# The scan layer's tile loop, six turns of two tiles, written out on all five engines

## The reference, cut to what matters

```
h = x @ fc1_w.T + fc1_b
xc, z = split(h @ in_proj_w.T, 2)            # 512 inner channels each
u = silu(causal_conv4(xc) + conv_b)
dt_low, Bm, Cm = split(u @ x_proj_w.T)       # 16, 16 states, 16 states
dt = softplus(dt_low @ dt_proj_w.T + dt_proj_b)
A = -exp(A_log)
hstate = exp(dt_t * A) * hstate + (dt_t * u_t) * B_t     # along the 2048 rows
y_t = einsum('bdn,bn->bd', hstate, C_t)
y = (y + u * D) * silu(z)
s = (y @ out_proj_w.T) @ fc2_w.T + fc2_b
g = silu((silu(xn @ wg.T) * (xn @ wu.T)) @ wd.T)
out = x + s * silu_of_ffn                    # silu_of_ffn = g above
```

## Time and profile before

| what | value |
|---|---|
| three timed runs | 3019.51, 3020.09, 3027.25 us, median 3020.09 |
| profiled execution | 3014.55 us |
| its span, from first to last instruction | 3012.9 us |
| scan layer in it | 1015 to 3012 us |
| busy over the span | PE 86%, DVE 77%, POOL 69%, ACT 67% |
| instruction queues | 127 and 109 packets, 2.08 and 0.89 MB |
| mean granted PE clock in the scan layer | 0.97 of full speed |

### The profile page before, as it was taken

How to read it: one execution, slowest core, us unless ns; L and a number is a source line. 1 busy time by engine, 2 the same in 40 slices (tenths; PEclk the granted TensorE clock), 3 DMA queues, 4 the chain that set the end, 5 groups by cost and what they waited for, 6 DMA issues and landing times.

```text
span 3012.9 us, 43961 instructions
## 1 busy us (share of the span) xinstructions
PE 2588.0 (86%) x13290; PEld 1488.0 (49%) x13290; DVE 2306.4 (77%) x2777; ACT 2027.6 (67%) x3268; POOL 2069.9 (69%) x650
## 2 busy tenths in 40 slices
PE   6776188888887769998999899999899899999987
PEld 2333033333333435564665555656556566566455
DVE  6577466556562269989889799898798888989995
ACT  3221146656564379878788698797787887978874
POOL 0454430000000179999999899999899999999996
PEclk9998579989998879999999999999999999999999
DMA  8335497767641123032132130321312303213210
GB/s 274 105 103 127 109 266 210 186 175 180 172 140 46 55 120 120 30 119 100 36 120 85 65 120 33 117 99 36 121 52 97 120 17 126 105 38 120 78 63 7
DMA packets 133934, 323.21 MB, mean 107 GB/s; under 512 B 13233, under 2 KB 89009, under 8 KB 117314
## 3 DMA queue, kind: packets, MB, share of 16 engines
q1 hardware_dynamic: 113186, 248.84, 26.7%
q0 software_dynamic: 19200, 70.73, 7.1%
q10 hardware_dynamic: 1312, 0.66, 0.1%
HBM read 277.12 MB, written 43.13 MB: 106 GB/s over the span
## 4 chain that ended last, share of the span: by engine, by line
PE 26%; issue 12%; POOL 12%; ACT 7%; DVE 7%; ACTq 1%; DVEq 1%; DMA 0%; POOLq 0%; SPq 0%
PE l_p_w L1995 11%; PE l_p_y L1987 6%; POOL l_st L1638 5%; PE l_p_w L2041 5%; DVE l_st L1457 4%; POOL l_st L1630 3%; PE l_p_w L2060 3%; ACT l_p_a L1716 2%; POOL keep_xg L1638 2%; DVE keep_xg L1457 1%; ACT L1791 1%; POOL l_dtu L1644 1%; ACT L1725 1%; DVE keep_xg L1466 1%; PE l_p_w L2017 1%
## 5 line engine op out<-in xcount | busy, mean ns | idle before, releaser
L1457 DVE TENSOR_TENSOR_SCAN l_st<-l_p_a,l_hl,l_st 128x512 f32<-128x512 f32 x768 | 931.6, 1265 | 112.1 <-ACT l_p_a L1716 93.0
L1638 POOL TENSOR_TENSOR l_st<-l_st,l_cs 128x2048 f32<-128x2048 f32 x192 | 868.6, 4541 | 4.1 <-ACT l_hl L1721 3.8
L1716 ACT ACTIVATE l_p_a<-l_dt,lw_a_neg 128x512 f32<-128x512 f32 x1024 | 666.1, 681 | 51.6 <-DVE keep_xg L1457 40.4
L1630 POOL TENSOR_TENSOR l_st<-l_bs,l_dtu 128x2048 f32<-128x2048 f32 x128 | 580.9, 4539 | 47.5 <-PE l_p_y L1987 44.2
L1987 PEld LDWEIGHTS l_p_y<-keep_ident,l_st 128*128 128x128 f32 x3072 | 353.8, 144 | 136.9 <-POOL l_st L1638 74.8
L1987 PE MATMUL l_p_y<-keep_ident,l_st 128*128 128x128 f32 x3072 | 382.4, 281 | 42.9 <-POOL l_st L1638 42.9
L977 ACT ACTIVATE a_pr<-a_p_s 128x512 f32<-128x512 f32 x512 | 284.8, 596 | 163.9 <-PE a_p_s L1043 145.7
L901 DVE TENSOR_REDUCE a_mpart<-a_p_m 128x1 f32<-128x512 f32 x512 | 315.2, 683 | 98.2 <-PE a_p_m L1008 96.5
L1457 DVE TENSOR_TENSOR_SCAN keep_xg<-l_p_a,l_hl,keep_xg 128x512 f32<-128x512 f32 x256 | 314.8, 1267 | 2.3 <-DVE keep_xg L1466 1.9
L1638 POOL TENSOR_TENSOR keep_xg<-keep_xg,l_cs 128x2048 f32<-128x2048 f32 x64 | 290.7, 4542 | 11.0 <-ACT l_hl L1721 11.0
L1043 PE MATMUL a_p_s<-a_qst,kx 99*128 99x256 bf16 x1024 | 206.7, 292 | 73.6 <-ACT a_pr L977 54.8
(11 more groups left out here) (225 smaller groups left out, 3920.1 us busy)
## 6 DMA issues: line engine op xcount, KB each, us to landing
a_w<-in_w_dram POOLq DMA_DIRECT2D x64, 1024.0 KB, 12.0
l_bs<-s_bc SPq DMA_DIRECT2D x64, 1024.0 KB, 4.7
l_cs<-s_bc SPq DMA_DIRECT2D x64, 1024.0 KB, 4.9
keep_share<-s_x SPq DMA_DIRECT2D x32, 512.0 KB, 4.4
s_kp<-t_kp SPq DMA_DIRECT2D x96, 128.0 KB
kx<-s_kp SPq DMA_DIRECT2D x16, 768.0 KB, 11.8
s_vp<-t_vo SPq DMA_DIRECT2D x16, 544.0 KB
a_vg<-s_vp SPq DMA_DIRECT2D x16, 544.0 KB, 11.7
```

The costliest lines, as they stand in the source:

```text
L1457: eng.tensor_tensor_scan(st[k % NG][:, n, :], p_a[:, n, :], st[k % NG][:, n, :], hl[:, k, n:n + 1], ALU.mult, ALU.add).then_inc(scan_ok, 1)
L1630: eng.tensor_tensor(st[n][:, :, :], bs[:, 4 * n:4 * n + 4, :], dtu[(k // NG) % 2][:, :].unsqueeze(1).broadcast_to([P, NG, TT]), ALU.mult). ...
L1638: eng.tensor_tensor(st[n][:, :, :], st[n][:, :, :], cs[:, 4 * n:4 * n + 4, :], ALU.mult).then_inc(cm_ok, 1)
L1716: eng.activation(p_a[:, n, :], dt[c % 2][:, :], ACT.Exp, scale=a_neg[:, c, m:m + 1]).then_inc(dA_ok, 1)
```

## The change

The loop is gone. All 19 periods, -1 to 17, are written out by a loop of the program that builds the kernel, so that q is a plain number everywhere. For each q the four flags and the parity have the same values as before; on each engine the operations of a period and their order are the same.

```diff
--- before.py
+++ after.py
@@ -66,16 +66,8 @@
 
 def tiles(eng, period):
 
-    period(-1, 1, False, False, False, True)
-    period(0, 0, True, False, False, True)
-    period(1, 1, True, True, False, True)
-    with eng.Fori(0, (NT - 4) // 2) as j:
-        for p in range(2):
-            period(j * 2 + (2 + p), p, True, True, True, True)
-    period(NT - 2, 0, True, True, True, True)
-    period(NT - 1, 1, True, True, True, False)
-    period(NT, 0, False, True, True, False)
-    period(NT + 1, 1, False, False, True, False)
+    for q in range(-1, NT + 2):
+        period(q, q % 2, 0 <= q < NT, 1 <= q <= NT, 2 <= q, q + 1 < NT)
```

## The result

| | before | after |
|---|---|---|
| median of the timed runs | 3023.67 us (4 runs, 3019.51 to 3027.87) | 2975.09 us (4 runs, 2972.40 to 2976.80) |
| profiled execution, its span | 3014.55, 3012.9 us | 2973.50, 2971.8 us |

The ratio of after to before is 0.9838, with a 95% interval from 0.9818 to 0.9859: faster by 1.6%.

A forecast was written before the change was run, and what follows sets the result against it. POOL, almost without slack, was taken to bound the scan layer. Jumps 30.4 and register work 11.0 (41.35 by row spacing) plus 0.6 for period 2 gave 42 us: 3020.1 - 42.0 = 2978 us, range 2967 to 2991.

The forecast's parts named there:

- POOL sets the pace, and the written-out tiles 14 and 15 are the measure: Scan layer: POOL is busy 115.39 of 118.10 us per loop tile; the twelve loop tiles should become like periods 14 and 15.
- Jumps, 30.4 us: Scan loop: five jumps back stall PE and lengthen their tiles by 3.3 to 9.7 us each; all 30.4 us go.
- Register work, 1.03 us a tile: Scan loop tiles: computed waits and their arithmetic cost 118.06 - 117.03 us per tile, 11.0 us over eleven tiles.
- Period 2's first half, 0.6 us: Before the first residual row counted: POOL's wait should fall from 2.40 to 1.77 us, gaining 0.6.
- Straight code costs nothing to fetch: Twelve new written-out tiles: instruction traffic falls and no fetch stall is added, as in tiles 14 and 15; cost zero.
- rival (c): Slower: PE stalls at 16 KB packet ends in straight code, 48 packets, 149 us against 42 gained, 3127 us; chance 0.04.
- the DVE row: Straight code: one unexplained 3.00 us on DVE, taken as costing nothing; far bound 36 us if all twelve tiles exposed one.
- (a): Scan tiles: only the jumps go, the 1.03 us per tile stays; gain 30.4 us, time 2990; chance 0.06.
- (b): Scan layer: PE's stalls come from something else at a new turn and stay; gain 11.6 us, time 3008; chance 0.03.
- The clock: Granted PE clock: expected to lose its dip to 0.96 in the tile with the longest stall.
- the tile that was named: The scan loop tile with the longest PE stall, 5.09 us; the tile takes 127.71 us.
- The base: Whole kernel: the 42.0 us gain was put against the median 3020.1 of three timed runs, giving 2978.

The follow-up runs named there:

- PE's loop alone: Against the kernel before: PE keeps the loop of six turns, the four other engines are written out; 3011.42 us, ratio 0.9976.
- four periods a turn: Against the kernel before: three turns of four periods on every engine instead of six of two; 2997.12 us, ratio 0.9927.
- the hint: Kernel before, loop kept, plus one instruction per turn and engine naming the jump back ahead of time; 2987.47 us, ratio 0.9901.
- ACT's loop alone: Against the kernel before: ACT keeps the loop of six turns, the four other engines are written out; 2987.89 us, ratio 0.989.

## Why the prediction was right, by its own steps

- **POOL sets the pace, and the written-out tiles 14 and 15 are the measure.** Right: 117.03 us expected for each tile, 117.03 measured; 41.35 us for the eleven, 41.33 measured.
- **Jumps, 30.4 us.** Right in size and bearer, and shown three ways: PE's loop alone makes the five tiles as long again, two jumps instead of five (four periods a turn) cost 12 us instead of 30, and the hint removes it. Of the five engines it is PE's jump alone that costs much; the prediction had read that from the rows but not claimed it. One part of the mechanism it left unsaid: the stalls are 21.3 of the 30.4 us. The rest is the lower clock level at four of the five jumps, where PE does half the work. Stall plus half of that stretch gives 4.8, 6.5, 3.4, 10.2 and 6.6 us (an estimate from the trace), and the tiles' excess over 118.06 is 4.79, 6.36, 3.34, 9.65 and 6.21. With four periods a turn it gives 5.1 and 6.6, where the tiles exceed their neighbours by 5.1 and 6.6; with PE's loop alone it gives 1.3 to 1.6 us too much at four of five jumps.
- **Register work, 1.03 us a tile.** The gain per tile was right, its make-up was not. The bearer was not named: I argued over PE's wait, but PE's own share is zero; it waits for ACT's copy. ACT's loop alone costs 0.83. And a loop tile without a stretch at the lower clock level takes only 117.7, so the register work by itself is 0.7; the other 0.3 comes only where such a stretch falls into a loop tile. The 0.83 of ACT alone is more than the 0.7 of all five engines together, so the parts don't add up exactly.
- **Period 2's first half, 0.6 us.** The wait fell by 0.62 as said, but the row came 1.44 earlier. The rest stands ahead of it, in code that the change doesn't touch, and it is scatter: in the ten kernels whose attention stage is the same, this first row lies between 1224.76 and 1229.87.
- **Straight code costs nothing to fetch, rival (c).** Right: no stall over 1 us in twelve more tiles, on any engine, but the DVE row, which is there again at its old place (2.99 us). It is not open any more:

```profile
2838.65 4.55 POOL L1622 TENSOR_TENSOR l_st<-l_bs,l_dtu 128x2048 f32<-128x2048 f32 x1
...
2843.29 1.28 DVE L1449 TENSOR_TENSOR_SCAN l_st<-l_p_a,l_hl,l_st 128x512 f32<-128x512 f32 x1 [2.99 <-issue]
```

  DVE starts 0.09 us after POOL has finished the product that this scan works on (2838.65 + 4.55 = 2843.20). It waited for POOL and the profile did not name it. That a stretch is marked "issue" is no proof of a fetch.
- **Rivals (a) and (b).** Both fell: all tiles shortened, and the stalls went with the jumps. By the figure of the Trainium skill, "Advanced Engine Details and Errata", section Control Flow Timing, about 108 ns for a compare-and-branch, the jumps would have cost next to nothing and (b)'s time would have held; the trace disagrees, with 3.10 to 5.09 us at each, 29 to 47 times that figure.
- **The clock.** Right for the tile that was named, but it was left out for the rest. The stretches at the lower level at four of the five jumps are gone, others remain at other places, and one costs 1.7 us in the interval from period 15 to 16, which the prediction had put at nothing. With this 1.7 less and 0.8 more at the start, the spans differ by 41.1 us, not 42.
- **The base.** 2978 was 3 us high, and that it came so close is partly luck: the gain between the medians was forecast as 42.0. The medians differ by 48.6 us, the profiled executions by 41.05 (ratio 0.9864, just outside of the interval). The kernel before scatters: 3009.10 to 3030.94 us in 14 runs, and the one with PE's loop alone over 14 us, while the written-out kernel keeps within 5.2. The profiled execution was among the cheap ones. The scatter goes with the granted clock: of 28 runs of the kernel before, taken beside the others, the nine with a mean of 0.940 or 0.941 took 3009 to 3022 us and the six with 0.935 or 0.936 took 3022 to 3031. Within one trace a jump's cost differs from 3.3 to 9.7 us by its packets and its stretch at the lower level, so it may well differ between executions too; there is only one trace of the kernel before, so this is argued and not shown.

## What to carry to other kernels

Look in a trace for a stall without a named reason on the first instruction behind a loop's jump back. Where the engine that it hits feeds the one without slack, write the loop out, or name the jump ahead; one engine at a time shows which stream matters. A written-out tile elsewhere in the same kernel is the best measure of what a loop's tile will become. A wait against a computed value costs rows of its own, and the engine whose rows delay the chain can be one with a third of its time free, as ACT here.

## What the runs showed of the hardware that I had not expected

- In the scan layer a taken jump back costs PE 2.6 to 5.1 us before its first product (twelve jumps in three traces), whether the turn has two periods or four, and 5.5 and 5.8 us in the attention stage of the kernel before. At eleven of the twelve, the first four products then run partly at the lower clock level (2.83 to 3.78 us against 1.88). Compares that are not taken, and branches to what comes next, cost nothing measurable. The Trainium skill, "Runtime: NRT & Kernel Launch", section Instruction fetch mechanics, says that a taken branch out of the fetched window waits for its page; the trace agrees, with these numbers.
- Behind each of these jumps lies a 16 KB packet of q8, and the product starts 1.65 to 1.82 us after it has landed. A hint at the top of the turn brings the packet ahead of the jump: it took the stall away in nine of ten jumps of the scan layer's loop in two traces, and left 2.28 us in one.
- In the kernel after, the granted PE clock falls to the lower level for 3.4 us eight times between 1200 and 2850 us, without any stall. Seven of these POOL does not notice; the eighth costs 1.7 us. Elsewhere such a stretch costs 1.3 to 1.7 us at the start of a tile or ahead of the product that POOL waits for, and 0.3 to 0.5 in a loop tile without a jump.
